# A transformer block with a one-token shift: the residual stream held shifted, each writer writing two halves

## The reference

```python
h = _layernorm(x) * (1 + ca) + sa
x = x + ga * attn_ref(h, guidance)          # windowed differences against 64 guides
h = _layernorm(x) * (1 + cb) + sb
x = x + gb * ffn_ref(h, ...)                # two layers as below

def _layer(x, ...):
    h = shift_token(x)                      # dims 64..127 come from the token before
    q, k, v = split(h @ wqkv)               # 8 heads of 64; q, k to unit length, rotated
    x = x + local_attention(q, k, v) @ wo   # windows of 64 tokens
    h = shift_token(x)
    h = layernorm(h) * lg + lb
    a, g = split(h @ w1 + b1)
    return x + (a * gelu(g)) @ w2 + b2
```

## Time and profile before

| | us |
|---|---|
| median of 3 runs | 1008.69 (1006.82 to 1008.88) |
| the profiled execution's span, first to last instruction | 1004.1 |
| PE busy | 786.4 (78%), 7119 instructions |
| VectorE busy | 698.4 (70%), 1659 |
| ScalarE busy | 652.1 (65%), 1539 |
| GpSimd busy | 545.9 (54%), 1116 |
| chain that ended last, by engine | PE 37%, DVE 21%, ACT 16%, issue 15%, POOL 9% |

### The profile page before, as it was taken

One profiled execution on the slowest core, in us unless ns is written; L12 is line 12 of the kernel. 1 busy time (PEld: TensorE's weight loads), 2 busy tenths in 40 slices (PEclk: granted clock), 3 DMA queues, 4 the chain that ended last, 5 costly groups with the idle time before them and its releaser, 6 DMA issues.

```text
span 1004.1 us, 21260 instructions
## 1 busy us (share of the span) xinstructions
PE 786.4 (78%) x7119; PEld 556.9 (55%) x7151; DVE 698.4 (70%) x1659; ACT 652.1 (65%) x1539; POOL 545.9 (54%) x1116
## 2 busy tenths in 40 slices
PE   3344678797979797797979788898879787979974
PEld 3223456565656575565656565565656565656642
DVE  4466586494997794485897796494998765676742
ACT  1133474686876694686867685686786766867752
POOL 3146472373876481383786483373876563474601
PEclk9657699999999898999999999999999999999996
DMA  6000000000000000000000000000000000000000
GB/s 198 0 1 0 11 1 12 1 2 1 2 2 2 23 2 25 1 2 2 2 1 2 22 3 22 1 1 2 1 2 1 12 2 11 2 2 1 3 7 15
DMA packets 12298, 10.05 MB, mean 10 GB/s; under 512 B 1040, under 2 KB 11288, under 8 KB 12184
## 3 DMA queue, kind: packets, MB, share of 16 engines
q1 hardware_dynamic: 12184, 8.64, 2.8%
HBM read 6.54 MB, written 2.10 MB: 9 GB/s over the span
## 4 chain that ended last, share of the span: by engine, by line
PE 37%; DVE 21%; ACT 16%; issue 15%; POOL 9%; DMA 1%; POOLq 0%; SPq 0%; ACTq 0%; DVEq 0%
ACT probs L738 7%; PE pair L463 6%; PE dense L600 4%; DVE space L1176 3%; DVE q_norm L1179 3%; PE mixed L494 3%; PE dense L563 3%; POOL h_lo L1263 3%; PE dense L564 3%; PE dense L565 2%; PE dense L678 2%; PE pair L526 2%; DVE space L1174 2%; POOL qk L1288 2%; ACT squares L856 2%
## 5 line engine op out<-in xcount | busy, mean ns | idle before, releaser
L1288 POOL TENSOR_TENSOR qk<-space 128x512 f32<-128x512 f32 x128 | 197.3, 1554 | 28.6 <-DVE q_norm L1179 23.9
L738 ACT ACTIVATE probs<-pair,neg_max 128x128 f32<-128x128 f32 x512 | 138.5, 386 | 19.8 <-DVE neg_max L992 19.5
L1176 DVE TENSOR_TENSOR space<-dense,tables 128x512 f32<-128x512 f32 x128 | 87.3, 682 | 44.0 <-ACT space L860 44.0
L678 PE MATMUL dense<-wq_hi,h_hi 128*128 128x512 f32 x192 | 92.8, 483 | 21.5 <-DVE space L1176 12.2
L1285 POOL TENSOR_TENSOR space<-space,tables 128x512 f32<-128x512 f32 x64 | 84.2, 1316 | 30.9 <-ACT space L860 30.9
L856 ACT ACTIVATE squares<-dense 128x512 f32<-128x512 f32 x128 | 77.4, 605 | 34.0 <-PE dense L680 33.0
L463 PE MATMUL pair<-eye_s,probs 128*128 128x128 f32 x512 | 78.4, 286 | 26.0 <-ACT probs L738 26.0
L992 DVE TENSOR_REDUCE neg_max<-pair 128x4 f32<-128x512 f32 x128 | 82.1, 683 | 17.8 <-PE pair L526 17.6
L1179 DVE TENSOR_REDUCE q_norm<-squares 128x8 f32<-128x512 f32 x128 | 86.4, 675 | 0.0
L1277 POOL TENSOR_TENSOR h_lo<-shifted,h_hi 128x512 fp32r<-128x512 f32 x16 | 20.3, 1266 | 121.2 <-DVE h_hi L1163 121.2
L463 PEld LDWEIGHTS pair<-eye_s,probs 128*128 128x128 f32 x512 | 58.7, 145 | 46.6 <-ACT probs L738 44.0
(11 more groups left out here) (175 smaller groups left out, 1966.1 us busy)
## 6 DMA issues: line engine op xcount, KB each, us to landing
x_in<-n_L_attn_embeddings_dram SPq DMA_DIRECT2D x8, 256.0 KB, 3.2
out_dram<-hn SPq DMA_DIRECT2D x8, 256.0 KB, 2.5
qk<-in_L_ffn_wqkv_dram SPq DMA_DIRECT2D x1, 1536.0 KB, 6.2
qk<-in_L_ffn_w_dram SPq DMA_DIRECT2D x1, 682.0 KB, 7.5
wo_s<-in_L_ffn_wo_dram SPq DMA_DIRECT2D x2, 256.0 KB
o_t<-in_L_wmod_dram SPq DMA_DIRECT2D x1, 384.0 KB, 3.4
probs<-const_rotary_dram SPq DMA_DIRECT2D x1, 256.0 KB, 3.7
band_s<-const_band_dram SPq DMA_DIRECT2D x1, 256.0 KB, 7.8
```

What stands on the lines that cost most here:

```text
L678: pe.matmul(to[:, :], h_hi[:, rows], wq_hi[:, layer, cols], start=True, stop=False)
L738: last = act.activation(probs[:, ring, hh, :], banks[m][:, hh * P:(hh + 1) * P], ACT.Exp, bias=neg_max[:, ring, hh:hh + 1], scale=1.0)
L1176: dve.tensor_tensor(turned_s[:, t % 2, m, :].rearrange("p (h a b) -> p h a b", h=HEADS, a=2), halves[:, :, ::-1, :], rot(layer, t, 2 * m + 1),
L1288: pool.tensor_tensor(qk[s][:, t, m * INNER:(m + 1) * INNER], turned_c[:, t % 2, m, :], turned_s[:, t % 2, m, :], ALU.add).then_inc(added, 1)
```

## The change

Tile `shifted`, both helpers' copies and two semaphores go. y_new and y_t get one more column per sequence (257), and are held so that columns 0 to 255 read on all partitions are the shifted stream: partitions 0 to 63 hold token n at column n, partitions 64 to 127 at column n+1, and column 0 is set to zero once. Whoever touches the stream unshifted works on two halves of the partitions with different column ranges; whoever reads it shifted reads columns 0 to 255.

```diff
+        HALVES = (slice(0, P // 2), 0), (slice(P // 2, P), 1)
+        def at_token(tile, dims, late):
+            return tile[dims, :, late:late + SEQ]
+        def shifted(tile):
+            return tile[:, :, 0:SEQ]
...
# PE, ff.stats
-                    pe.wait_ge(ff_shifted, before + 1)
+                    pe.wait_ge(attended, att_upto)
...
# ScalarE: shift() and its two callers go
-                act.activation(shifted[0:P // 2, :, :], src[0:P // 2, :, :], ACT.Copy)
-                act.activation(shifted[P // 2:P, :, 1:SEQ], src[P // 2:P, :, 0:SEQ - 1], ACT.Copy).then_inc(done_sem, 1)
...
# ScalarE, new.stream (L805) and store.scale (L881), for each sequence b
-                        last = act.activation(to[:, b, :], src[:, b * SEQ:(b + 1) * SEQ], ACT.Identity,
+                        for dims, late in (HALVES if what == "stream" else ((slice(0, P), 0),)):
+                            last = act.activation(to[dims, b, late:late + SEQ], src[dims, b * SEQ:(b + 1) * SEQ], ACT.Identity,
...
-                        last = act.activation(hn[:, b * SEQ:(b + 1) * SEQ], y_t[stream(slot)][:, b, :], ACT.Copy,
+                        for dims, late in HALVES:
+                            last = act.activation(hn[dims, b * SEQ:(b + 1) * SEQ], y_t[stream(slot)][dims, b, late:late + SEQ],
...
# VectorE, a.project (L984) and ff.down (L1061)
-                    dve.tensor_tensor(flat(y_t[s]), flat((y_t if layer else y_new)[s]), mixed[:, :],
-                                      ALU.add).then_inc(attended, 1)
+                    for dims, late in HALVES:
+                        last = dve.tensor_tensor(at_token(y_t[s], dims, late), at_token((y_t if layer else y_new)[s], dims, late),
+                                                 by_seq(mixed[dims, :]), ALU.add)
...
+                    for dims, late in HALVES:
+                        y = at_token(y_t[stream(slot)], dims, late)
+                        last = dve.scalar_tensor_tensor(y, by_seq(src[dims, :]), columns[dims, row:row + 1], y, ALU.add, ALU.add)
...
# VectorE, proj.split (L1163): waits that ScalarE's shift had
-                    dve.wait_ge(qkv_shifted, before + 1)
-                    dve.tensor_copy(h_hi[:, :], flat(shifted)).then_inc(qkv_hi, 1)
+                    if slot == 2 and runs(i, 1, step, turns):
+                        dve.wait_ge(*filled_at(i, 1, (PROJ, "tile", TILES - 1, 2)))
+                    dve.tensor_copy(by_seq(h_hi[:, :]), shifted((y_t if slot < 2 else y_new)[s])).then_inc(qkv_hi, 1)
```

## The result

The changed kernel takes 1036.47 us (median of 4 runs, 1034.73 to 1037.02) and the kernel before 1007.76 (median of 4, 1003.94 to 1008.88). The ratio is 1.0279, with a 95% interval of 1.0246 to 1.0313. The forecast was 1034.1 with a range of 1021 to 1041.

The account below looks back on a forecast made before the run. No engine is full; chains from engine to engine set the time. Terms 14.9 + 5.4 + 1.4 + 0.9 + 2.8 = 25.4 us added to the 1008.7 median gave 1034.1, range 1021 to 1041.

Parts of the forecast that it names:

- (a): End of slots 2 and 3, with a store: halved y_t and hn delay PE's turn and x's load, 8 x 1.86 = 14.9 us.
- (b): Down product of slots 0 and 1: second y_t half delays o_rows, PE's turn and o_t, 8 x 0.67 = 5.4 us.
- The 0.2 of slack on PE: Down product, slots 0 and 1: PE busy about 0.2 us longer than o_rows, so 0.67 of the delay reaches its turn.
- (c): Slot 0 to 1: half and root meet GpSimd's products, statistics and maxima come 0.35 later, 4 places, +1.4 us.
- its rival: Slot 0 to 1: ScalarE's lead from the removed copy comes through, 4 x -0.8 = -3.2 us; total 1029.5, chance 0.12.
- (d): Slot 1 to 2: the added y_t half delays half, root, h_hi and h_lo by 0.3 at 3 places, +0.9 us.
- (e): Output projection between up products, slots 2 and 3: added y_t half delays PE's down product, 7 x 0.4 = +2.8 us.
- slack: Rival: short waits in the slots absorb (b), (c) and (e), leaving 14.9 + 0.9; 1024.5 us, chance 0.22.
- the copies of h_hi: Upper rival: VectorE's h_hi copies lose pace, 14 x 0.28 = 3.9 us, and more GpSimd meetings; 1038.0, up to 1041, chance 0.12.
- halves were not worked side by side: Rival claimed the opposite: lower and upper halves run simultaneously, so (a), (b), (d), (e) cost nothing; 1003.9 us, chance 0.04.
- at most 4.8: Only gain worked out from removing ScalarE's shifted copies, between slots 0 and 1: 3.2 to 4.8 us.

Follow-up runs that it names:

- g1: Kernel before plus one wait: in slots 0 and 1 VectorE multiplies qk by root only once GpSimd has written h_lo; 981.18 us.
- g5: g2 plus 24 identity turns on PE at each of the 8 stores, issued while PE waits for hn; 1008.29 us.
- e1: Changed kernel with the stream written and read on whole tiles, no copies, the shift left out of the computation; 990.87 us.
- g7: e1 with the wait of g1, and y_t after the output projection written in two halves, 16 times; 984.89 us.
- g8: g2 with the four pieces of hn written lower, lower, upper, upper instead of lower, upper, lower, upper; one run, 1013.87 us.
- g2: Changed kernel with the same added wait as g1; 1013.51 us.
- e2: e1 with hn on ScalarE written in halves of the partitions, four pieces instead of two, at 8 stores; 1004.11 us.

## Why the prediction was right

The direction, the range and nearly the size hold, and the step that carried most held by its own marks. That the number came within 2.4 us is in part luck. In the profiles the terms make 33.0 from the first down product on, where 25.4 stood. The start, which the change hardly touches, takes 2.7 off. And the distance from the profiled span to the median, which the prediction left at 4.6, is 2.1 after the change, because the profiled execution of before was a short one: a run's own time lies only some 1.8 above its span.

- (a) was right as a mechanism: hn in four pieces of 0.505 over 2.06, eight times, 1.92 to PE's turn instead of 1.86, ScalarE's saved copies eaten by the halves of y_new. It led the delay through the load of x, though, and that is waited for at only two of the 8 stores; at the others PE's own queue carries it on. Whether all 1.92 come through each time is not shown: from g1 to g5 the stretches behind the stores of slot 2 in turns 1 and 2 grow by only 1.18 and 1.14. There the issue of x's load took 0.46 and 0.38 in g5 and 1.03 and 1.35 in g1, which is most of the difference. What it missed is behind the store: the longer wait drops PE's clock. g5 shows that at these stores.
- (b) was worked out at 0.67 and measured at 0.72 to 0.79 at all 8 places. The 0.2 of slack on PE was misread: PE's turn of o_rows had started at their end, and o_t came 0.89 later.
- (c) was right in its first step, +0.38 to +0.59 for +0.35, and so was the price of its rival: e1's plain passages gain 0.9 where 0.8 stood. Where the passage ends goes with where the low clock falls (24.19 to 23.52, but 24.38 to 26.10); this was read off four passages and not tested.
- (d) and (e) were right in sign and low by 0.8 and 0.9. g7 has these and (c) together at 10.1 for 9.0.
- The rivals: slack did not take (b), (c) and (e), or 1024.5 would have come; the copies of h_hi kept their pace; halves were not worked side by side (2.06 for four of 0.505, and g8). Each of them was told apart by a row that the prediction had named.

One thing was not in the prediction at all and is larger than most that was: eight times an order at the ports of VectorE and GpSimd, worth 27 us, which both kernels lose. It did not move the comparison, since in its profile neither wins it even once. But in e1's profile the removal of the copies alone wins two of the eight, some 7 of its 17.6 us. A forecast for e1 made in the same way, 1004.6, was wrong by 13.7. So the terms of the halves held roughly, while the claim that the removed copies are worth at most 4.8 did not hold for the kernel as it was: there they gain 17.6. With the order fixed it is 6.4, which the spread doesn't tell from 4.8.

Open: the distance from g1 to g2 is 32.3 and from before to after 28.7. That they differ is not shown: the interval of the second is 24.8 to 31.5, that of the first about 29 to 34, and in the profiles it is the other way round (26.6 and 30.3). Open too are about 5 of the 10 us that the halves cost beyond their worked-out 28.6, once the fill has given back 5.2, and about 7 of e1's 17.6, beyond the two won orders and the lead at four places. Last, why single runs of one kernel differ so much: e2 runs from 999.71 to 1008.92, but g2, where the order at these eight places is fixed, has six runs from 1008.97 to 1012.09 and six from 1014.93 to 1017.04. Their mean granted clock doesn't tell them apart (0.918 to 0.924 and 0.921 to 0.927).

## What to carry to other kernels

Halving the partitions halves no time: an edit that turns one instruction into two on a path where the next engine waits cost the full second instruction here, and taking work off an engine gave something back only where the next step waited for that work, as in (c). Before costing a change, look for places where VectorE and GpSimd start within a few tenths of a microsecond of each other, and fix that order with a wait in favour of the one that PE waits for; until that is done, any small shift can gain or lose microseconds that look like its own doing. Price a longer wait of PE twice, once for its length and once for the clock behind it: here 3.4 us of idle time at a store instead of 1.5 cost its own 1.9 and, by g5, some 0.6 more.

## What the runs showed of the hardware

- An instruction of GpSimd that lost the order took 3.24 us instead of 1.26, and VectorE's 2048-element product 3.35 instead of 2.29 where it lost. With a wait in its favour (g1) GpSimd's took 1.26 again, and VectorE idled 1.37 at a place where nothing waited for it.
- ScalarE, too, started a piece early only behind one with the same first partition: 1.82 against 2.06 for the same four pieces.
- PE at half clock took 3.62 for sixteen turns that take 1.91. Twenty-four turns with no use, put where PE idled 3.4 us, brought the granted clock behind three stores from 0.77, 0.91 and 0.83 up to 1.00, and the kernel with them took 5.2 us less.
